# A transformer decoder layer on one core: keys by split products in rows, probabilities turned in other banks

## The chip, the cores and the metric

One Trainium2 chip, one of its cores. The metric is the device time of one execution in microseconds; lower is better. The kernel before takes 476.71 us (median of 3 runs, 476.16 to 478.13).

## What is computed

```python
x = x + xattn(layernorm(x), ctx_1024, fside, mask)   # 16 heads of 32, 4 x 128 queries, 4 x 2048 keys, 512 wide
x = x + attn(layernorm(x))                           # self attention with clamps
x = x + ffn(layernorm(x))                            # 8 experts, each takes its best 32 tokens of a batch, 512-2048-512, gelu
# xattn: q = t @ Wq.T + bq;  k, v = m @ Wkv.T + b;  softmax(q k / sqrt(32) + bias + pad) v @ out_w.T + out_b
```

All is float32. The padding mask lets through only the keys at the end of each batch's context, so that of the 64 chunks of 128 keys only those that hold such a key need any work: 11 chunks with these inputs.

## The kernel before

The instructions of each engine are written out by hand in one block per engine, and semaphores order them. There is no planner: the order in each engine's block is the order of its work.

**Split products.** Where a product needs more than one rounding to the matmul's fast 32-bit type (`F32R`), both operands are held as a high half (a cast, by ScalarE) and a low half (operand minus high half, by VectorE), and TensorE adds three products: high by high, high by low, low by high. `split_att(n)` (L411 on ScalarE, L678 on VectorE) does that for one 512x512 weight matrix, `split_chunk(t)` (L471, L732) for the context chunk `ctx_s`, `project_t` and `project` (L1133, L1150) use the halves. `k_project` (L1098) doesn't: it multiplies plain float32, `wk_s` by `ctx_s`, in 16 matmuls of 128 columns, each of which the trace shows as two records, and gets the keys already turned (features in partitions).

**Start.** x is loaded and normalised, turned by TensorE (`turn_batch`), and the queries of all 512 rows are projected (`project_t`, 4 groups of 12 matmuls of 512 columns, into PSUM banks 0 to 3). VectorE evacuates each group twice (`queries`, L748): 128 columns for the first batch into `q_now`, and all 512 into `qt`. VectorE also adds the output bias to x (L758), four instructions. `scores(0)` waits for all of `q_now` and `q_out`. After it come the values of chunk 0 (`v_project`, L1107, four blocks of 3 matmuls of 512 columns into bank 5).

**Chunk loop.** Z below is the start of `scores` of a chunk. In `chunk(t)` (L1216) TensorE does, in this order: keys of chunk t+1 (bank 4, `pk`), the turning back of the attended values of chunk t-1 (`turn_values`, L1209), and then blocks of the values of t+1 between the turning of the probabilities of t (`turn_probs`, L1188, a group of four heads each), `scores(t+1)` (L1167) and `values(t)` (L1195). Probabilities are turned in place: into the score banks 0 to 3 they came from, and VectorE (groups 0 to 2, L803) and ScalarE (group 3, `turned_last`, L439) copy them to `big_b`. So `scores(t+1)`, which writes the same banks, waits for all of these copies. ScalarE's order (L452): exponents of groups 0 and 1 (8 pairs of instructions), the copy of the attended values (`turned_out`, L434), the rescaling factor, exponents of groups 2 and 3, `turned_last`, and the cast of the next context chunk. VectorE's order (`chunk`, L834): two maxima of 8 heads each (L784) with the new running maximum (L787), values evacuated (L729), context low half (L735), changes of the maxima (L792, L794), attended values added to the state (L813), keys evacuated with their bias (L740), state rescaled (L801), turned probabilities 0, 1, 2 (L806), sums (L818, L821). GpSimd copies the queries of the next chunk's batch to `q_now` after each `scores` (L367). SyncE loads the mask rows and the next context chunk; the SyncE and ScalarE queues each issue loads of their own.

`chunk(t)` is run once for t = 0, in a hardware loop for 8 chunks (t = 1 to 8), and once more for the last but one chunk (t = 9) with the normalisation of the first two batches mixed in (`at_end`). A tail (L873 on) does the last chunk together with the output projection of the cross attention. Then come self attention, the routing, and the eight experts, whose weight tiles (`w_tile`, 1 MB each) are loaded by SyncE over the attention's weights (L297 for the first expert) and first cast by ScalarE in `split_first` (L530).

PSUM banks 0 to 3 are `ps`, 4 is `pk`, 5 `pv`, 6 and 7 `po[:, 0]` and `po[:, 1]`. `turn_values` writes bank 7.

## Time and profile before

| | |
|---|---|
| median of 3 runs | 476.71 us |
| the profiled execution | 477.78 us, of which its span is 476.1 us |
| PE busy | 436.1 us (92%) |
| VectorE busy | 371.5 us (78%) |
| ScalarE busy | 294.0 us (62%) |
| GpSimd busy | 81.3 us (17%) |
| bytes moved | 81.99 MB, mean 172 GB/s |

The span goes from the first to the last recorded instruction of one profiled execution; the device time has 1.7 us around it. A matmul's record ends when its result is written, and the next one starts before that: the pace of a row of matmuls is read from the starts. The start, with the first scores, takes until about 33 us, the chunks until about 156 us, the rest of the attention until about 247 us, the routing until 266 us, and the experts the rest.

### The profile page before, as it was taken

What the parts mean: (1) busy time and instruction counts of PE and PEld (TensorE: products, weight loads), DVE (VectorE), ACT (ScalarE), POOL (GpSimd) and SP (SyncE); (2) the same over time, 40 slices, a digit from 0 to 9 for tenths busy, and PEclk for the clock granted to TensorE, in tenths of its full rate; (3) what the DMA queues carried; (4) which work ended last, traced back from release to release, by engine and by line L of the source; (5) the groups of instructions that cost most, each with busy time, mean ns of one, the idle gap of its engine ahead of it and who ended that gap; (6) DMA issues with size and microseconds to landing.
All of it is one profiled execution on the core that took longest, in us unless ns stands there. A gap on an engine that the chain in (4) does not pass through costs nothing. (4 is left out here: it accounts for less than half of the span.)

```text
span 476.1 us, 9610 instructions
## 1 busy us (share of the span) xinstructions
PE 436.1 (92%) x3323; PEld 361.0 (76%) x3323; DVE 371.5 (78%) x500; ACT 294.0 (62%) x600; POOL 81.3 (17%) x88
## 2 busy tenths in 40 slices
PE   1979999999998999989966799999999999999993
PEld 1858888888887779878855688787878787878782
DVE  5796666777778885758877779898989898898963
ACT  1436666666666743567240587778787878777752
POOL 5000000000000022000133141323223140505000
PEclk9999999999999999999987999999999999999998
DMA  8891100000000742610000099999999999898002
GB/s 258 285 337 36 24 24 22 22 22 22 22 22 2 252 147 89 198 70 3 0 2 0 22 393 387 386 381 356 334 348 322 344 319 380 290 382 296 0 0 88
DMA packets 42959, 81.99 MB, mean 172 GB/s; under 512 B 3000, under 2 KB 3128, under 8 KB 42936
## 3 DMA queue, kind: packets, MB, share of 16 engines
q1 hardware_dynamic: 38744, 75.85, 45.5%
q10 hardware_dynamic: 4192, 5.83, 3.7%
q8 instruction: 14, 0.23, 0.2%
q14 instruction: 9, 0.07, 0.0%
HBM read 80.58 MB, written 1.10 MB: 172 GB/s over the span
## 5 line engine op out<-in xcount | busy, mean ns | idle before, releaser
L1059 DVE TENSOR_TENSOR w_lo<-att_w,w_hi 128x2048 fp32r<-128x2048 f32 x60 | 137.8, 2306 | 23.4 <-ACT w_hi L604 23.4
L604 ACT CAST w_hi<-att_w 128x2048 fp32r<-128x2048 f32 x60 | 115.0, 1917 | 15.4 <-PE po L1421 15.4
L426 ACT ACTIVATE big_a<-ps,negm 128x128 f32<-128x128 f32 x176 | 62.4, 406 | 21.0 <-DVE negm L787 21.0
L1421 PE MATMUL po<-w_hi,ht_hi 128*128 128x512 f32 x128 | 51.8, 405 | 0.0
L1421 PE MATMUL po<-w_hi,ht_lo 128*128 128x512 f32 x128 | 50.6, 395 | 0.0
L1421 PE MATMUL po<-w_lo,ht_hi 128*128 128x512 f32 x128 | 50.5, 394 | 0.0
L426 ACT ACTIVATION_READ_ACCUMULATOR big_a<-ps,negm 128x1 f32 x176 | 43.4, 247 | 0.0
L1104 PE MATMUL pk<-ctx_s,att_w 128*128 128x128 f32 x352 | 42.1, 278 | 0.3 <-DMA ctx_s<-in_ctx_t 0.3
L1104 PEld LDWEIGHTS pk<-ctx_s,att_w 128*128 128x128 f32 x352 | 40.2, 192 | 2.4 <-issue 2.3
L784 DVE TENSOR_REDUCE mc<-ps 128x8 f32<-128x1024 f32 x22 | 26.8, 1220 | 12.4 <-PE ps L1185 12.4
L1421 PEld LDWEIGHTS po<-w_hi,ht_lo 128*128 128x128 f32 x128 | 24.1, 188 | 5.7
L1421 PEld LDWEIGHTS po<-w_lo,ht_hi 128*128 128x128 f32 x128 | 24.1, 188 | 5.1
L1421 PEld LDWEIGHTS po<-w_hi,ht_hi 128*128 128x128 f32 x128 | 24.1, 188 | 5.0
L367 POOL COPY q_now<-qk 128x512 f32 x10 | 6.6, 662 | 124.0 <-PE ps L1185 124.0
L1421 PE MATMUL pv<-w_hi,xin_hi 128*128 128x512 f32 x64 | 26.0, 406 | 1.5 <-DVE w_lo L927 1.5
L1421 PE MATMUL pk<-w_hi,xin_hi 128*128 128x512 f32 x64 | 26.2, 410 | 0.3 <-DVE xin_lo L1048 0.3
L399 POOL CAST back_now<-state 128x128 fp32r (+1 forms) x8 | 8.6, 1075 | 101.5 <-PE ps L1461 87.6
L1421 PE MATMUL pv<-w_hi,xin_lo 128*128 128x512 f32 x64 | 25.3, 395 | 0.0
L1421 PE MATMUL pk<-w_hi,xin_lo 128*128 128x512 f32 x64 | 25.3, 395 | 0.0
L1421 PE MATMUL pv<-w_lo,xin_hi 128*128 128x512 f32 x64 | 25.2, 394 | 0.0
L1421 PE MATMUL pk<-w_lo,xin_hi 128*128 128x512 f32 x64 | 25.2, 394 | 0.0
L1192 PE MATMUL ps<-ident,big_a 128*128 128x128 f32 x176 | 24.4, 272 | 0.0
(284 smaller groups left out, 983.2 us busy)
## 6 DMA issues: line engine op xcount, KB each, us to landing
att_w<-in_w SPq DMA_DIRECT2D x64, 1024.0 KB, 6.5
ctx_s<-in_ctx_t SPq DMA_DIRECT2D x11, 256.0 KB, 2.6
x_s<-in_x SPq DMA_DIRECT2D x4, 256.0 KB, 3.6
att_w<-in_wq SPq DMA_DIRECT2D x1, 1024.0 KB, 8.4
att_w<-in_wk SPq DMA_DIRECT2D x1, 1024.0 KB, 10.8
att_w<-in_wv SPq DMA_DIRECT2D x1, 1024.0 KB, 8.4
att_w<-in_sv ACTq DMA_DIRECT2D x1, 1024.0 KB, 7.9
att_w<-in_wo ACTq DMA_DIRECT2D x1, 1024.0 KB, 7.5
```

What stands on the lines that cost most here:

```text
L367: g.tensor_copy(q_now[:], qt[:, bass.ds(b, 1)].rearrange("p a k n -> p (a k) n")).then_inc(q_staged, 1)
L399: g.tensor_copy(back_now[:], back[:, bass.ds(e, 1), :].rearrange("p a n -> p (a n)")).then_inc(back_staged, 1)
L426: ins = a.activation(big_a[:, h], ps[:, c, g * P:(g + 1) * P], ACT.Exp, bias=negm[:, h:h + 1], accum_out=sums[:, h:h + 1])
L604: a.copy(w_hi[:, i % SLOTS], att_w[:, i]).then_inc(hi_ok, 1)
L784: v.tensor_reduce(mc[:, hs], ps[:, 2 * half:2 * half + 2].rearrange("p c (g k) -> p (c g) k", k=P), AX.X, ALU.max).then_inc(loop_dve, 1)
L1059: v.tensor_tensor(w_lo[:, i % SLOTS], att_w[:, i], w_hi[:, i % SLOTS], ALU.subtract).then_inc(lo_ok, 1)
L1104: ins = mm(pk[:, g * P:(g + 1) * P], wk_s[:, k, g * P:(g + 1) * P], ctx_s[:, k], start=k == 0, stop=k == KC - 1)
L1192: ins = nc.tensor.transpose(ps[:, c, g * P:(g + 1) * P], big_a[:, c * KC + g], ident[:])
L1421: ins = mm(dst, l, r, start=start and i == 0, stop=i == len(terms) - 1, skip_group_check=True)
```

## The change

Names of weight halves. `att_r` lies on the same bytes as `att_w`: the halves of the key weights go where the query and key weights were, those of the output weights where the value and output weights were.

```diff
+        att_r = halves.enter_context(nc.sbuf_tensor("att_r", [P, 8, KC, D], F32R))
+        keys_s = att_w[:, 6, 1]
+        wk_hi, wk_lo, wo_hi, wo_lo = (att_r[:, i] for i in range(4))
-        SPLITS = ((wq_s, 2, in_wq), (wv_s, 1, in_wv), (sv_s, 3, in_sv), (wo_s, 2, in_wo), (sq_s, 1, in_sq), (sk_s, 0, in_sk), (so_s, 1, in_so))
+        SPLITS = ((wq_s, slot_of(2), in_wq), (wk_s, (wk_hi, wk_lo), in_wk), (wv_s, slot_of(1), in_wv), (sv_s, slot_of(3), in_sv),
+                  (wo_s, (wo_hi, wo_lo), in_wo), (sq_s, slot_of(1), in_sq), (sk_s, slot_of(0), in_sk), (so_s, slot_of(1), in_so))
+        TURNED_PROBS = [7, 4, 7, 4]
```

SyncE, the tiles of the first expert; and GpSimd, ahead of its loop:

```diff
             sp.wait_ge(v_mm, last + 2)
-            sp.wait_ge(att_lo_ok, 4)
-            for i in range(2 * NQ):
+            for i in (0, 1, 4, 2, 3, 5, 6, 7):
                 if i == 4:
-                    sp.wait_ge(att_lo_ok, 5)
+                    sp.wait_ge(att_lo_ok, 6)
+                if i == 2:
+                    sp.wait_ge(o_mm, B)
...
             pool.wait_ge(q_out, 4)
+            pool.wait_ge(in_bo, 16)
+            for b in range(B):
+                g.tensor_tensor(x_s[:, b], x_s[:, b], bo_b[:], ALU.add).then_inc(bo_added, 1)
```

ScalarE before its loop. All weight loads are now issued one after the other, and it makes the full query tiles. In `split_att`, split 1 (keys) waits for the low half of the query weights, split 4 (output) for that of the value weights.

```diff
             load_att(sv_s, sv, in_sv)
-            split_att(1)
             load_att(wo_s, wo, in_wo)
-            split_att(2)
...
-            act.wait_ge(q_mm, KC)
+            split_att(1)
+            split_att(2)
+            def queries(c):
+                act.wait_ge(q_first, c + 1)
+                a.activation(qt[:, :, c], ps[:, c].rearrange("p (b t) -> p b t", b=B), ACT.Identity,
+                             bias=bq_scaled[:, c:c + 1], scale=SCALE).then_inc(q_out, 1)
+            act.wait_ge(bq_ok, 1)
+            queries(0)
             split_att(3)
+            queries(1)
+            split_att(4)
+            queries(2)
+            queries(3)
             split_chunk(1)
```

VectorE before its loop (the low half of the key weights also waits for the first keys) and in `chunk`:

```diff
+            def keys_evacuate(t):
+                dve.wait_ge(k_mm, t + 1)
+                v.tensor_copy(keys_s, pk[:]).then_inc(keys_ok, 1)
...
-                v.tensor_scalar(qt[:, :, c], ps[:, c].rearrange("p (b t) -> p b t", b=B), cols[:, 0, c:c + 1],
-                                SCALE, ALU.add, ALU.mult).then_inc(q_out, 1)
+            split_chunk(0)
+            dve.wait_ge(in_cols, 80)
+            v.tensor_scalar(bq_scaled[:], cols[:, 0], SCALE, None, ALU.mult).then_inc(bq_ok, 1)
+            split_att(1)
             queries(0)
-            dve.wait_ge(in_bo, 16)
-            for b in range(B):
-                ins = v.tensor_tensor(x_s[:, b], x_s[:, b], bo_b[:], ALU.add)
-            link(ins)
+            split_att(2)
+            k_evacuate(0)
             queries(1)
-            split_att(2)
+            split_att(3)
             queries(2)
             queries(3)
-            split_att(3)
+            split_att(4)
...
                 nm = running(neg_max, t)
+                if before is None:
+                    v_evacuate(t)
+                split_chunk(t + 1)
                 maximum(t, nm, 0)
                 maximum(t, nm, 1)
                 if before is not None:
                     dve.wait_ge(pv_mm, t)
-                v_evacuate(t)
-                split_chunk(t + 1)
+                    v_evacuate(t)
                 moved_maxima(t, nm)
+                keys_evacuate(t + 1)
                 if before is not None:
                     add_values(before, t)
                 k_evacuate(t + 1)
+                turned_probs(t, 0, banks[TURNED_PROBS[0]])
+                turned_probs(t, 1, banks[TURNED_PROBS[1]])
                 rescale(t, running(state, t))
...
```

The old places of probabilities 0 and 1 in `chunk` go; 2 and the sums stay behind the rescaling, and in the `at_end` chunk the reciprocals stand between the rescaling and 2. `k_evacuate` now waits for `kt_mm`, the turned keys. TensorE: `k_project(0)` is the old product under the name `first_keys`; the others are new.

```diff
+            def k_project(t):
+                pe.wait_ge(ctx_lo_ok, t + 1)
+                pe.wait_ge(k_out, t)
+                if isinstance(t, int) and t == 1:
+                    pe.wait_ge(att_lo_ok, 2)
+                else:
+                    pe.wait_ge(pt_act, t - 1)
+                product(pk[:], [(c[:, k], w[:, k]) for k in range(KC)
+                                for c, w in ((ctx_hi, wk_hi), (ctx_hi, wk_lo), (ctx_lo, wk_hi))]).then_inc(k_mm, 1)
+            def turn_keys(t):
+                pe.wait_ge(keys_ok, t)
+                for g in range(KC):
+                    ins = nc.tensor.transpose(pk[:, g * P:(g + 1) * P], keys_s[:, g * P:(g + 1) * P], ident[:])
+                ins.then_inc(kt_mm, 1)
...
-                if not isinstance(t, int) or t > 0:
-                    pe.wait_ge(pt_dve, t * 3)
-                    pe.wait_ge(pt_act, t)
...
+            def turn_aside(t, c):
+                if c == 0 and (not isinstance(t, int) or t > 0):
+                    pe.wait_ge(pt_dve, t * 3)
+                if c == 1:
+                    pe.wait_ge(k_out, t + 2)
+                if c >= 2:
+                    pe.wait_ge(pt_dve, t * 3 + (c - 1))
+                turn_probs(t, c, banks[TURNED_PROBS[c]])
...
                 k_project(t + 1)
+                v_project(t + 1, 0)
                 if before:
                     turn_values(t)
-                v_project(t + 1, 0)
-                turn_probs(t, 0)
                 v_project(t + 1, 1)
-                turn_probs(t, 1)
+                turn_keys(t + 1)
+                turn_aside(t, 0)
                 v_project(t + 1, 2)
-                turn_probs(t, 2)
-                turn_probs(t, 3)
+                turn_aside(t, 1)
+                turn_aside(t, 2)
+                turn_aside(t, 3)
                 v_project(t + 1, 3)
                 scores(t + 1)
...
+            pe.wait_ge(att_lo_ok, 3)
+            for k in range(KC):
+                v_project(0, k)
             pe.wait_ge(q_out, 4)
             scores(0)
-            pe.wait_ge(att_lo_ok, 2)
-            for k in range(KC):
-                v_project(0, k)
```

`turn_values` now writes bank 6 (`po[:, 0]`), and `values(t)` waits for `summed` instead of `ot_out`. In the tail the probabilities are still turned in their own banks, and `cross_project` takes the output weights' halves from their new place.

## Rows read from the trace of the kernel before

**Rows 1.** Timeline, GpSimd: the query copies that follow scores 1 and 9
```profile
48.63 0.61 POOL L367 COPY q_now<-qk 128x512 f32 x1 [12.88 <-PE ps L1185]
...
141.47 0.61 POOL L367 COPY q_now<-qk 128x512 f32 x1 [10.99 <-PE ps L1185]
```
**Rows 2.** Timeline, PE, chunk 1: start us, us, instruction, [idle before <-releaser]
```profile
47.15 0.40 PE L1180 MATMUL ps<-bias,ones 32*128 32x512 bf16 x4
...
49.38 3.84 PE L1104 MATMUL pk<-ctx_s,att_w 128*128 128x128 f32 x32
53.51 0.66 PE L1213 MATMUL po<-ident,att_w 128*128 128x128 f32 x4 [0.29 <-ACT att_w L437]
53.92 0.48 PE L1114 MATMUL pv<-w_hi 128*128 128x512 f32 x1
54.24 0.39 PE L1114 MATMUL pv<-w_lo,w_hi 128*128 128x512 f32 x1
...
54.70 0.60 PE L1192 MATMUL ps<-ident,big_a 128*128 128x128 f32 x4
...
56.97 1.03 PE L1192 MATMUL ps<-ident,big_a 128*128 128x128 f32 x8
57.76 0.47 PE L1114 MATMUL pv<-w_hi 128*128 128x512 f32 x1
...
58.77 0.40 PE L1180 MATMUL ps<-bias,ones 32*128 32x512 bf16 x4
```
**Rows 3.** Timeline, VectorE and then ScalarE, the same chunk
```profile
48.50 1.22 DVE L784 TENSOR_REDUCE mc<-ps 128x8 f32<-128x1024 f32 x1 [1.33 <-PE ps L1185]
...
52.03 0.68 DVE L735 TENSOR_TENSOR w_lo<-ctx_s,w_hi 128x512 fp32r<-128x512 f32 x1
52.63 0.17 DVE L792 TENSOR_TENSOR mdiff<-negm,neg_max 128x16 f32<-128x16 f32 x1
...
57.60 0.69 DVE L806 COPY big_b<-ps 128x512 f32<-128x512 f32 x1 [0.21 <-PE ps L1192]
...
50.08 0.37 ACT L426 ACTIVATE big_a<-ps,negm 128x128 f32<-128x128 f32 x1 [2.35 <-DVE negm L787]
...
52.83 0.63 ACT L437 COPY att_w<-po 128x512 f32<-128x512 f32 x1
...
58.04 0.59 ACT L441 COPY big_b<-ps 128x512 f32<-128x512 f32 x1 [1.68 <-PE ps L1192]
58.73 0.62 ACT L475 CAST w_hi<-ctx_s 128x512 fp32r<-128x512 f32 x1
```
**Rows 4.** Timeline, PE, start: first query matmul, scores 0, a value matmul behind it
```profile
18.83 0.50 PE L1130 MATMUL ps<-tr_hi,w_hi 128*128 128x512 f32 x1 [0.16 <-DVE tr_lo L676]
...
33.14 0.40 PE L1180 MATMUL ps<-bias,ones 32*128 32x512 bf16 x4 [2.89 <-DVE qk L752]
...
34.71 0.63 PE L1114 MATMUL pv<-w_lo,w_hi 128*128 128x512 f32 x1
```
**Rows 5.** Stretch 34 to 39 us: busy by engine, clock (0.66), DMA share, GB/s
```profile
34.00:39.00 5.00, 5.00 (x30) 3.93 (x27) 3.89 (x5) 0.00 (x0) 1.10 (x1) 0.66 0.44 151
```
**Rows 6.** One line's instructions: duration ns min/median/max, first and last start
```profile
L415 ACT CAST w_hi<-att_w x7: 1899/1910/1912, 11.2 to 195.8; 128x2048 fp32r<-128x2048 f32 x7
L682 DVE TENSOR_TENSOR w_lo<-att_w,w_hi x7: 2276/2282/2293, 14.1 to 197.7; 128x2048 fp32r<-128x2048 f32 x7
```
**Rows 7.** The same view of a GpSimd line, and one VectorE row beside it
```profile
L387 POOL TENSOR_TENSOR tr_lo<-norm,tr_hi x4: 1261/1270/3191, 247.5 to 253.6; 128x512 fp32r<-128x512 f32 x4
...
252.31 1.21 DVE L1021 TENSOR_TENSOR gsm<-gsm,gred 128x32 f32<-128x32 f32 x1
```
**Rows 8.** Timeline of the tail: PE scores 10, VectorE maximum, PE second turning
```profile
152.53 0.39 PE L1180 MATMUL ps<-bias,ones 32*128 32x512 bf16 x4 [1.02 <-DVE big_b L806]
...
153.90 1.23 DVE L784 TENSOR_REDUCE mc<-ps 128x8 f32<-128x1024 f32 x1 [0.46 <-PE ps L1185]
...
156.09 0.66 PE L1123 MATMUL pk<-ident,norm 128*128 128x128 f32 x4 [0.67 <-DVE tr_lo L676]
```
**Rows 9.** Expert tile loads (KB, us to landing); their fifth issue; first use of tile 2
```profile
att_w<-in_w SPq DMA_DIRECT2D x64, 1024.0 KB, 6.5
...
178.91 0.37 SPq L306 DMA_DIRECT2D att_w<-in_w  x1
...
201.38 1.90 ACT L534 CAST w_hi<-att_w 128x2048 fp32r<-128x2048 f32 x1
```

More of the change, by code:

```diff
@@ L69, in decoder_layer @@
         cols = sb("cols", [P, 4, KC])
+        bq_scaled = sb("bq_scaled", [P, KC])
         gate_s = sb("gate_s", [P, KC, E])
@@ L411, in split_att @@
             def split_att(n):
-                w, slot, landed = SPLITS[n]
+                w, halves, landed = SPLITS[n]
                 act.wait_ge(landed, 16)
-                a.copy(w_hi[:, slot], w).then_inc(att_hi_ok, 1)
+                if n == 1:
+                    act.wait_ge(att_lo_ok, 1)
+                if n == 4:
+                    act.wait_ge(att_lo_ok, 3)
+                a.copy(halves[0], w).then_inc(att_hi_ok, 1)
             def transposed(i, b):
@@ L437, in turned_out, with turned_last @@
                 a.copy(ot_s[:].rearrange("p k t -> p (k t)"), po[:, 0]).then_inc(ot_out, 1)
-            def turned_last(t):
+            def turned_last(t, bank):
                 act.wait_ge(pt_mm, 4 * t + 4)
-                a.copy(big_b[:, 3 * KC:4 * KC].rearrange("p h k -> p (h k)"), ps[:, 3]).then_inc(pt_act, 1)
+                a.copy(big_b[:, 3 * KC:4 * KC].rearrange("p h k -> p (h k)"), bank).then_inc(pt_act, 1)
             def turned_second(t):
@@ L459, in softmax_chunk @@
                 exponents(t, 3)
-                turned_last(t)
+                turned_last(t, banks[TURNED_PROBS[3]])
             act.dma_start(mask_s[:], key_mask).then_inc(in_mask, 16)
@@ L509, in _ @@
             normed_cross(0)
-            turned_last(last)
+            turned_last(last, ps[:, 3])
             transposed(2, 0)
@@ L812, in add_values @@
                 dve.wait_ge(loop_dve, 4 * n)
-                v.tensor_tensor(st, st, po[:, 1], ALU.add).then_inc(summed, 1)
+                v.tensor_tensor(st, st, po[:, 0], ALU.add).then_inc(summed, 1)
             def add_sums(t):
@@ L851, in chunk @@
                     reciprocals(0, 2)
-                turned_probs(t, 1)
+                turned_probs(t, 2, banks[TURNED_PROBS[2]])
                 if at_end:
                     attended(0)
-                turned_probs(t, 2)
                 add_sums(t)
@@ L881, in _ @@
             cross_output(0)
-            turned_probs(last, 0)
+            turned_probs(last, 0, ps[:, 0])
             add_values(prev, last)
@@ L886, in _ @@
             reciprocals(2, 3)
-            dve.wait_ge(pt_mm, 4 * last + 3)
-            v.tensor_copy(big_b[:, 2 * KC:3 * KC].rearrange("p h k -> p (h k)"), ps[:, 2]).then_inc(pt_dve, 1)
+            turned_probs(last, 2, ps[:, 2])
             attended(2)
@@ L902, in _ @@
             transposed(1, 3)
-            split_att(4)
+            split_att(5)
             cross_output(3)
@@ L1096, in _, with first_keys @@
             mm = nc.tensor.matmul
-            def k_project(t):
-                pe.wait_ge(ctx_in, t * 16 + 16)
-                if not isinstance(t, int) or t > 0:
-                    pe.wait_ge(k_out, t)
+            def first_keys():
+                pe.wait_ge(ctx_in, 16)
                 for g in range(KC):
@@ L1148, in project_half, with project @@
                         ins.then_inc(done, 1)
-            def project(slot, b, dst, done):
+            def project(halves, b, dst, done):
                 now = slice(b * T, (b + 1) * T)
-                product(dst, [(t[:, k, now], w[:, slot, k]) for k in range(KC)
-                              for w, t in ((w_hi, tr_hi), (w_lo, tr_hi), (w_hi, tr_lo))]).then_inc(done, 1)
+                hi, lo = halves
+                product(dst, [(t[:, k, now], w[:, k]) for k in range(KC)
+                              for w, t in ((hi, tr_hi), (lo, tr_hi), (hi, tr_lo))]).then_inc(done, 1)
             prime(pe, v_mm, s_mm)
@@ L1186, in scores, with turn_probs @@
                 ins.then_inc(s_mm, 1)
-            def turn_probs(t, c):
+            def turn_probs(t, c, bank):
                 pe.wait_ge(p_ok, t * 4 + (c + 1))
                 for g in range(KC):
-                    ins = nc.tensor.transpose(ps[:, c, g * P:(g + 1) * P], big_a[:, c * KC + g], ident[:])
+                    ins = nc.tensor.transpose(bank[:, g * P:(g + 1) * P], big_a[:, c * KC + g], ident[:])
                 ins.then_inc(pt_mm, 1)
+            def turn_aside(t, c):
[6 more added lines that the diff above has]
+                turn_probs(t, c, banks[TURNED_PROBS[c]])
             def values(t, at_end=False):
@@ L1212, in turn_values @@
                 for g in range(KC):
-                    ins = nc.tensor.transpose(po[:, 1, g * P:(g + 1) * P], ot_s[:, g], ident[:])
+                    ins = nc.tensor.transpose(po[:, 0, g * P:(g + 1) * P], ot_s[:, g], ident[:])
                 ins.then_inc(bt_mm, 1)
@@ L1236, in _ @@
             pe.wait_ge(in_wk, 16)
-            k_project(0)
+            first_keys()
             pe.wait_ge(tr_lo_ok[0], B)
@@ L1264, in _ @@
             pe.wait_ge(v_out, last + 1)
-            pe.wait_ge(att_lo_ok, 4)
+            pe.wait_ge(att_lo_ok, 5)
             cross_project(0)
-            turn_probs(last, 0)
-            turn_probs(last, 1)
+            turn_probs(last, 0, ps[:, 0])
+            turn_probs(last, 1, ps[:, 1])
             cross_project(1)
-            turn_probs(last, 2)
-            turn_probs(last, 3)
+            turn_probs(last, 2, ps[:, 2])
+            turn_probs(last, 3, ps[:, 3])
             turn_batch(2, 0)
```

57 lines of the change are left out of this document (31 added, 26 removed).

## The prediction

> **What bounds the kernel now.** The change touches the start and the chunk loop, so I read those and not the experts. First the GpSimd copies that follow each `scores` [rows 1]: from scores 1 at 48.63 to scores 9 at 141.47 there are 8 periods, (141.47 - 48.63) / 8 = 11.60 us a chunk. Then one chunk in the timelines, all measured from Z = 47.15, the start of `scores` [rows 2, 3]. The reader is to see that PE looks full and is not the limit. It waits for ScalarE's copy of the attended values before `turn_values` (0.29 us, at Z+6.36), and again ahead of the next scores. What sets the period is a chain:
>
> - Z to the first maximum, 1.35 (48.50); maximum to first exponent, 1.58 (50.08); eight exponents, 2.75 (52.83); copy to `turn_values`, 0.68 (53.51). So `turn_values` starts at Z+6.36, whatever PE did before.
> - From there PE works without a gap to the start of the last turning pair (56.97) and its end at 58.00; ScalarE copies group 3 at 58.04 until 58.63; scores at 58.77, Z+11.62. That leg is 5.26.
>
> **Step 1, keys as split products.** The plain product takes 3.84 us [rows 2]. The new one is 12 matmuls of 512 columns. Their pace is (54.70 - 54.24) / 2 = 0.23 us, a block of three takes 0.78 behind a transpose and 0.70 behind another block [rows 2]; so 12 take 0.32 + 11 x 0.23 = 2.85. The turning of the keys adds four transposes, 0.41 after a wait (53.51 to 53.92), about 0.4 in a row (0.79 for eight, 56.97 to 57.76). PE has 3.84 - 2.85 - 0.4 = 0.6 us less work a chunk. This saving lies ahead of the `turn_values` gate: keys end at Z+5.1, the first value block at Z+5.8, and PE then waits until Z+6.36 for ScalarE. All but the 0.29 us of today's wait is nothing gained, and those 0.29 don't set the gate either. Worth zero in the loop. The added key copy on VectorE (as the copy in rows 3, 0.60 from start to next start) stands at Z+5.3, in the stretch where VectorE now waits for `turn_values`; covered. If that cover went, it would add 0.6.
>
> **Step 2, the probabilities in banks 7 and 4.** Scores no longer wait for the copies; instead each turning waits for the bank's last reader. After the gate, PE goes: `turn_values` 0.41, value block 0.78, keys and group 0 turned 0.79, value block 0.78. So group 1 is turned at Z+6.36+2.76 = Z+9.12. Its bank is free: keys are evacuated from Z+8.2 to Z+8.9. VectorE can copy group 1 at 9.12 + 0.63 = 9.75 (four transposes 0.60, pick-up 0.03 as at 57.60 behind 56.97). Group 3 needs that bank: 9.75 + 0.69 + 0.07 = Z+10.51. The exponents of group 3 are done at about Z+9.2 (6.28 behind the first one), earlier, so the copy decides. Then 0.41 for turning, 0.78 for the last value block: next Z at 11.70. The leg behind the gate is 5.34 instead of 5.26: the copy wait is not removed, it is moved one value block forward, and it now goes through VectorE.
>
> **Step 3, context low half moved to the front of VectorE's chunk.** The last value block now runs straight into scores, so its end, which releases ScalarE's cast, comes at Z+0.17 instead of a little before Z (the cast starts at 58.73, 0.04 ahead of Z, now). Cast 0.62, then the subtraction, 0.60 of VectorE's time (52.03 to 52.63) [rows 3]: VectorE is free for the maximum at about Z+1.47, not Z+1.35. That is 0.12 on the chain. `k_project` waits for the low half too, until about Z+1.6, and is reached at Z+2.23 (49.38): covered.
> So the period is 11.70 + 0.12 = 11.82, and 8 periods cost 8 x 0.22 = +1.8 us. Bounds: the handoffs from VectorE to PE were taken as 0.07; if they are none and the subtraction hides, 11.6, +0; if each of the four between gate and scores costs 0.15 more, 12.4, +6.
>
> **Step 4, the start.** Before, PE ends the queries near 30.25 and sits idle 2.89 us until VectorE has evacuated them [rows 4]; after scores 0 at 33.14 the matmuls of the values start 0.43 apart instead of 0.23 (they last 0.63), in a stretch with granted clock 0.66 [rows 4, 5], that is partly at 1.2 GHz. Now the values of chunk 0 fill the gap: 18.83 + 48 x 0.2325 = 30.0, plus 12 x 0.23 = 32.8. Is all ready then? ScalarE issues its loads in one go until about 20.2, casts keys and values weights (1.91 each [rows 6]) by 24.1, makes query tile 0, casts the third by 27.3, and so on in turn; the last query tile is at 31.7. VectorE: key low half 22.1 to 24.4 (2.2 each [rows 6]), values low half by 26.9, third by 30.0, fourth until 32.8. Both in time: scores 0 at 32.8 against 33.14, at full clock. Next ScalarE casts chunk 1 from 33.0 and VectorE subtracts until 34.4, maximum at 34.35, exponents from 35.9. Sixteen exponents and the factor take 2 x 2.75 + 0.28 = 5.8: done 41.7, turning at 41.8, block, scores 1 at 43.0. Before it was 47.15 [rows 2]. Gain 4.15.
>
> **Step 5, x plus bias on GpSimd.** Four adds of 128x512 from 31.7 on. The nearest row is GpSimd's subtraction of that size, 1.27 us, and 3.19 where VectorE's 2.28 us subtraction ran first [rows 7]. The other way round, a VectorE instruction on 32 elements took 1.21 us while these ran [rows 7], some 1.0 more than its neighbours. So the adds run from 32.8 to about 38 and stand in the way of what VectorE does then: the subtraction, two small maxima steps and the change of maxima, all with two inputs in SBUF, all on the chain to the exponents. Nothing at best, 4 x 1.0 at worst; I take 1.0 in all, because VectorE's waits and GpSimd's gaps alternate. The gain of the start is 4.15 - 1.0 = 3.15. The adds themselves have until `cross_output`, 120 us later. The query copy behind them has until 43: covered.
> The Trainium skill, SBUF — State Buffer, Who interferes with whom, says that a VectorE instruction with two SBUF inputs contends with GpSimd reads, and that the order of issue decides who blocks. By that rule alone each of the four could meet an add, and the sum would be at its worst end, 479; the row shows one such meeting and not how often they come.
>
> **Step 6, the tail.** In the last but one chunk (Z at 139.99, 1.48 us ahead of its query copy at 141.47 [rows 1], as 47.15 is of 48.63) scores 10 now waits 1.02 us for the copies [rows 8]; this goes. But VectorE then sets the pace: probabilities 2 move behind rescaling and reciprocals, the key copy and the late front add up, and the maximum of chunk 10, today at Z+13.91, comes at Z+14.3 by the same steps. The second turning, today at Z+16.10, follows it: +0.4. Bounds -0.5 and +1. Loads of expert tiles: the fifth goes at 178.9, then 2 and 3; three at 6.5 each, even one after another, end by 198.4, before tile 2's cast at 201.38 [rows 9]. Zero; without that cover it would be 3 us at most. The cast and subtraction of the output weights merely change places; bq_scaled is four elements.
>
> **The sum.** -3.15 + 1.8 + 0.4 = -1.0 us. Against the profiled execution's own 477.78 that is 476.8; it lay 1.07 above the median, so on the median's scale 475.7.
>
> **Rivals.**
> A, faster: the loop doesn't lengthen and GpSimd meets VectorE rarely: -4.15 + 0 + 0.4 = -3.75, 473.0. For it: PE really has 0.6 us less to do per chunk. Against: the chain through ScalarE to Z+6.36 is untouched, and PE waits there already. Chance 0.33.
> B, slower: the handoffs around banks 7 and 4 cost more. Group 2 waits for copy 0, group 3 for copy 1, keys for their copy, and each wait stands in PE's order ahead of the last value block and scores. With +0.6 a chunk on top of step 2 (12.4), -3.15 + 6.4 + 0.4 = +3.6, 480.3. It decides from a period of 12.3 on: 8 x 0.65 = 5.2 outweighs the start and leaves over 2.4. For it: the copies that had one late reader now have three in line. Against: a PE row follows its releaser by 0.05 to 0.1 in rows 2. Chance 0.12.
> C, the clock: PE's idle time a chunk grows from 0.5 to 1.2 us, in pieces up to 0.7. Against: the granted clock is 1.0 in the loop with today's gaps; only after 2.9 us idle did it fall. If it fell once in the loop, the pace 0.43 instead of 0.23 would cost 9 matmuls behind the gate 1.8 us, and 15 ahead of it 3.0 less the wait of 0.7: 4 us for each chunk, 480. Chance 0.05.
> The skill's TensorE: Matmul & The Clock Gate, HAM oscillation, reports micro-idles from cycling PSUM banks as a cause of re-throttling, and its Part 4 says that transposes don't count as busy. This chunk cycles banks and adds transposes, so that rule speaks for C; the trace of before, with 20 transposes a chunk at clock 1.0, doesn't bear it out.
> My own case, -1.0, has 0.5.
>
> **How the numbers follow.** A measurement of this kernel tells changes above about 0.5%, 2.4 us: faster is below 474.3, slower above 479.1. Case A is all faster (0.33), and my case reaches across that line in few of its values: faster 0.34. B and C are slower: 0.17. Same: 0.49. The predicted time is my case's, 475.7. The range takes in A's 473.0 with the bound of the tail (-0.5 more, 472.5) and reaches up to 479.2, half of the way into B: 472.5 to 479.2. What is left out is the worst of B and C and a start better than computed.
>
> **What would show it.** Right: scores 1 near 44; GpSimd's query copies 11.8 apart; PE idle 0.6 to 0.7 ahead of `turn_values` and 0.5 ahead of the turning of group 3, with VectorE's copy as releaser; the maximum 0.1 later behind Z; clock 1.0 from 18 us on. The small VectorE steps of chunk 0 at over 1 us beside GpSimd's adds. Wrong: query copies 11.3 apart or less (PE was the limit), or 12.3 and more (B); clock below 1 in the loop (C); scores 1 later than 46 (the start gained nothing).

## The result, and the profile after

The changed kernel takes 490.5 us (median of 4 runs, 489.17 to 492.67) against 476.46 for the kernel before in the same comparison (476.16 to 478.13): ratio 1.0295, 95% interval 1.025 to 1.034. It is 14 us slower where 1 us less was forecast; time and direction were both wrong. The profiled execution took 490.2 us with a span of 488.5, 12.4 us above the span before. Two executions of the runs below were slow ones (one of number 10, 1089.13 us, and one of the kernel before beside it, 506.11 us), and the medians and ratios given there leave them out. The busy times of the changed kernel, from the page:

```profile
PE 439.9 (90%) x3163; PEld 350.6 (72%) x3163; DVE 376.2 (77%) x504; ACT 298.8 (61%) x605; POOL 90.3 (18%) x92
```

TensorE's busy time has hardly grown (436.1 before): the time is in waits, and it splits at three landmarks, which the kernel before has in [rows 2], [rows 1] and [rows 8].

**The start, +4.66.** Timeline of ScalarE and of its DMA queue (ACTq), from the first cast of the context on:

```profile
17.20 0.62 ACT L493 CAST w_hi<-ctx_s 128x512 fp32r<-128x512 f32 x1 [0.81 <-issue]
...
18.63 0.78 ACTq L487 DMA_DIRECT2D att_w<-in_sq  x1
19.44 1.30 ACTq L487 DMA_DIRECT2D att_w<-in_sk  x1
20.78 4.35 ACTq L487 DMA_DIRECT2D att_w<-in_so  x1
25.15 2.76 ACTq L506 DMA_DIRECT2D gate_s<-in_gate  x1
28.01 1.91 ACT L433 CAST att_r<-att_w 128x2048 fp32r<-128x2048 f32 x1 [10.19 <-issue]
```

The number behind each start is the duration. The prediction let ScalarE issue its loads until about 20.2. The issue of `so` alone lasted 4.35 us and that of the gate 2.76; ScalarE stood still for 10.19 us, and the first weight cast came at 28.01. TensorE's timeline in the same stretch, and the table of windows (PE, PEld, VectorE, ScalarE, GpSimd, clock, DMA share, GB/s):

```profile
34.76 0.80 PE L1168 MATMUL pv<-w_hi 128*128 128x512 f32 x1 [3.42 <-DVE w_lo L714]
35.35 0.63 PE L1168 MATMUL pv<-w_lo,w_hi 128*128 128x512 f32 x1
...
40.18 0.39 PE L1232 MATMUL ps<-bias,ones 32*128 32x512 bf16 x4
...
51.81 0.40 PE L1232 MATMUL ps<-bias,ones 32*128 32x512 bf16 x4
```
```profile
34.00:39.00 5.00, 4.24 (x10) 3.37 (x11) 5.00 (x7) 4.48 (x5) 0.00 (x0) 0.50 0.29 89
```

The values of chunk 0 were to fill the idle 2.89 us of [rows 4]; they start behind 3.42 us of idle time, and then run 0.43 apart at clock 0.50, the lower level of 1.2 GHz, where [rows 5] had 0.66. Scores 0 come at 40.18 (33.14 before), scores 1 at 51.81 (47.15 before). Some of that is not the change's: the cast of the context, at 17.20 here, is at 16.10 in the trace before, and between 16.30 and 17.84 in the traces of the experiments, whose code is the same up to there. Against that anchor scores 1 come at +34.61 instead of +31.05: 3.56 us later, with the other 1.1 lying ahead of the change. Where starts are compared below, it is from this cast, called the anchor.

**The loop, +6.27.** GpSimd's query copies behind scores 1 and scores 9:

```profile
53.30 0.78 POOL L381 COPY q_now<-qk 128x512 f32 x1 [6.95 <-PE ps L1237]
...
152.41 0.86 POOL L381 COPY q_now<-qk 128x512 f32 x1 [11.42 <-PE ps L1237]
```

(152.41 - 53.30) / 8 = 12.39 us a chunk, against 11.60 [rows 1] and the forecast 11.82. One chunk, Z = 88.89, first VectorE, then ScalarE, then PE (as [rows 3] and [rows 2]):

```profile
90.21 0.69 DVE L767 TENSOR_TENSOR w_lo<-ctx_s,w_hi 128x512 fp32r<-128x512 f32 x1 [0.93 <-ACT w_hi L493]
90.82 1.22 DVE L819 TENSOR_REDUCE mc<-ps 128x8 f32<-128x1024 f32 x1
...
99.21 0.69 DVE L841 COPY big_b<-pk 128x512 f32<-128x512 f32 x1 [0.28 <-PE pk L1244]
```
```profile
89.00 0.62 ACT L493 CAST w_hi<-ctx_s 128x512 fp32r<-128x512 f32 x1
92.38 0.37 ACT L444 ACTIVATE big_a<-ps,negm 128x128 f32<-128x128 f32 x1 [2.76 <-DVE negm L822]
...
95.14 0.62 ACT L455 COPY att_w<-po 128x512 f32<-128x512 f32 x1
```
```profile
88.89 0.40 PE L1232 MATMUL ps<-bias,ones 32*128 32x512 bf16 x4
...
95.81 0.66 PE L1275 MATMUL po<-ident,att_w 128*128 128x128 f32 x4 [0.31 <-ACT att_w L455]
...
98.57 0.60 PE L1244 MATMUL pk<-ident,big_a 128*128 128x128 f32 x4
99.06 0.65 PE L1244 MATMUL po<-ident,big_a 128*128 128x128 f32 x4
100.03 0.65 PE L1244 MATMUL pk<-ident,big_a 128*128 128x128 f32 x4 [0.32 <-DVE big_b L841]
...
101.31 0.40 PE L1232 MATMUL ps<-bias,ones 32*128 32x512 bf16 x4
```

The reader is to see that ScalarE's cast ends at 89.62 and VectorE's subtraction, which waited for it, starts 0.59 later. The row names ScalarE as what ended its wait, but ScalarE had long been done; something else stood between (run 2). So the maximum comes at Z+1.93 instead of Z+1.35; the steps from there (1.56, 2.76, 0.67) are those of before, and `turn_values` starts at Z+6.92 instead of Z+6.36. The leg behind it is 5.50 instead of 5.26. Together +0.80.

**The tail, +1.16.** The second turning of the cross attention comes at 168.18, 17.26 behind scores 9 at 150.92, instead of 16.10 behind. VectorE's maximum of chunk 10 stands 2.19 ahead of it in both traces (153.90 to 156.09 in [rows 8]), so all of the 1.16 lies ahead of that maximum:

```profile
165.99 1.23 DVE L819 TENSOR_REDUCE mc<-ps 128x8 f32<-128x1024 f32 x1
```

It comes at Z+15.07 (Z = 150.92) instead of Z+13.91, and VectorE has no wait left ahead of it, where [rows 8] has one of 0.46. 4.66 + 6.27 + 1.16 = 12.09 of the 12.4 us of the span. The gate projection follows the second turning 80.88 us later here and 80.89 in the trace before; the other 0.3 lies behind it.

### The profile page after: what moved, and what is told of

It reads as the page before. It is cut to its first block and busy times, and to the rows that moved or that the text cites. A ratio compares the mean times of both kernels' runs of the same rounds, so it can differ in the third digit from the quotient of the medians.

```text
span 488.5 us, 9319 instructions
## 1 busy us (share of the span) xinstructions
PE 439.9 (90%) x3163; PEld 350.6 (72%) x3163; DVE 376.2 (77%) x504; ACT 298.8 (61%) x605; POOL 90.3 (18%) x92
## 5 line engine op out<-in xcount | busy, mean ns | idle before, releaser
L1168 PE MATMUL pv<-w_hi 128*128 128x512 f32 x44 | 21.4, 487 | 6.8 <-DVE w_lo L714 3.4
L381 POOL COPY q_now<-qk 128x512 f32 x10 | 9.1, 914 | 98.4 <-PE ps L1237 98.4
L1184 PE MATMUL pk<-att_r,w_hi 128*128 128x512 f32 x80 | 25.8, 403 | 0.8 <-DVE w_lo L767 0.8
L407 POOL COPY x_now<-qk 128x512 f32 x7 | 16.1, 2301 | 41.5 <-PE pv L1485 41.5
```

Of the source, the lines that this page charges most:

```text
L381: g.tensor_copy(q_now[:], qt[:, bass.ds(b, 1)].rearrange("p a k n -> p (a k) n")).then_inc(q_staged, 1)
L407: g.tensor_copy(x_now[:], now).then_inc(x_now_ok, 1)
L1168: ins = mm(pv[:], c[:, k], w[:, 1, k], start=k == 0 and c is ctx_hi and w is w_hi, stop=k == KC - 1 and c is ctx_lo, skip_group_check=True)
L1184: ins = mm(dst, l, r, start=n == 0, stop=n == len(pairs) - 1, skip_group_check=True)
```

## Experiments

Totals of one kernel spread over some 5 us, and the run's mean granted clock goes with them: in 31 runs of the kernel before the fastest, 473.19 us, had 0.988 and the slowest, 478.91, had 0.971. So each experiment is read by positions in its trace first and by its total second. A large part of the spread lies in code that no experiment touches: from the gate projection to the end the traces take between some 238.0 us (runs 2 and 3) and 242.7 (runs 5 and 9). The kernel before had medians of 476.11 beside runs 1 to 4 and 475.60 beside 5 to 8 and beside 9 to 11.

**1. The four loads spread between ScalarE's casts.**

```diff
-            for dst, w, landed in ((sq_s, sq, in_sq), (sk_s, sk, in_sk), (so_s, so, in_so)):
-                load_att(dst, w, landed)
-            act.dma_start(gate_s[:], gate.rearrange("(k p) e -> p k e", p=P)).then_inc(in_gate, 16)
             split_att(1)
             split_att(2)
+            load_att(sq_s, sq, in_sq)
...
             split_att(3)
+            load_att(sk_s, sk, in_sk)
             queries(1)
             split_att(4)
+            load_att(so_s, so, in_so)
             queries(2)
+            act.dma_start(gate_s[:], gate.rearrange("(k p) e -> p k e", p=P)).then_inc(in_gate, 16)
```

> The changed kernel with its last four ScalarE loads (two query-side weights, output weights, gate) issued one by one between the casts instead of in one row. Theory 1 (issue): ScalarE was held by its own load issues until 28.0 us (4.35 us for the fourth, 2.76 us for the gate), so casts, halves and scores 1 came late. Expected: key cast near 19 to 20 us, scores 1 at 44 us instead of 51.8, time 490.5 - 7.8 = about 483, loop period unchanged at 12.4. Rival (arrival): the weights themselves come later because all loads share the bandwidth; then the casts still wait for their loads and scores 1 moves by less than 3 us, 488 or more.

484.89 us (4 runs), ratio 1.0195 (1.0136 to 1.0254). Timeline of ScalarE and its queue:

```profile
17.80 1.90 ACT L433 CAST att_r<-att_w 128x2048 fp32r<-128x2048 f32 x1 [0.88 <-issue]
...
28.52 0.38 ACTq L487 DMA_DIRECT2D att_w<-in_so  x1
29.14 0.37 ACTq L522 DMA_DIRECT2D gate_s<-in_gate  x1
```

The same two issues last 0.38 and 0.37 us instead of 4.35 and 2.76, the first weight cast comes at 17.80, and scores 1 at 44.40, 28.10 behind the anchor: 6.5 us earlier than in the changed kernel. The period stays (12.38 against 12.39). ScalarE's held-up issues were the loss at the start. The total fell by 5.6 and not by the expected 7.8: behind the gate projection this trace takes 241.15 us, that of the changed kernel 239.44.

**2. Context low half ahead of the read of the chunk's table entry.** In the chunk VectorE first reads registers to find its row of `neg_max`; the subtraction was placed behind that.

```diff
-                nm = running(neg_max, t)
                 if before is None:
                     v_evacuate(t)
                 split_chunk(t + 1)
+                nm = running(neg_max, t)
                 maximum(t, nm, 0)
```

> The changed kernel with VectorE's subtraction of the context low half put ahead of the reading of the chunk's batch number (a load from the table in SBUF and address arithmetic) in each pass of the loop. Theory 2 (table read): the subtraction starts 0.6 us after ScalarE's cast because VectorE is still reading the table, which used to be covered by the wait for scores. Expected: the subtraction starts within 0.1 us of the cast's end, the maximum 1.4 to 1.5 us behind the start of scores instead of 1.93, period 11.9 instead of 12.4, time 490.5 - 4.5 = about 486. Rival (handoff): the 0.6 us are the wait on the semaphore or GpSimd's query copy; then nothing moves, 490.5.

486.33 us (4 runs), ratio 1.0221 (1.0165 to 1.0277). Query copies from 53.61 to 149.67, so the period is (149.67 - 53.61) / 8 = 12.01. Moving one line that computes nothing gives back 0.38 us a chunk. GpSimd's copies also last 0.61 again where they lasted some 0.98 (rows of 65.53 to 140.00 in the changed kernel).

**3. Both.**

> Both edits. If theories 1 and 2 hold and the two parts are independent: 490.5 - 7.8 - 4.5 = about 478, scores 1 at 44 us, period 11.9. By both rivals: above 487.

480.22 us (10 runs), ratio 1.0093 (1.0059 to 1.0128). The gains of runs 1 and 2 add up, 490.5 - 5.6 - 4.2 = 480.7; what was too high in the expected 478 was each of them. Scores 1 stand 28.06 behind the anchor, the period is 12.00. Timeline of ScalarE, then VectorE, then PE, Z = 81.48:

```profile
81.58 0.62 ACT L493 CAST w_hi<-ctx_s 128x512 fp32r<-128x512 f32 x1
```
```profile
82.23 0.69 DVE L768 TENSOR_TENSOR w_lo<-ctx_s,w_hi 128x512 fp32r<-128x512 f32 x1 [0.37 <-ACT w_hi L493]
82.98 1.23 DVE L820 TENSOR_REDUCE mc<-ps 128x8 f32<-128x1024 f32 x1
```
```profile
87.98 0.66 PE L1276 MATMUL po<-ident,att_w 128*128 128x128 f32 x4 [0.31 <-ACT att_w L455]
...
93.46 0.40 PE L1233 MATMUL ps<-bias,ones 32*128 32x512 bf16 x4
```

The subtraction now follows the cast by 0.03 (81.58 + 0.62 = 82.20), and the maximum stands at Z+1.50, the forecast being Z+1.47. It starts 0.75 behind the start of the subtraction, in the changed kernel 0.61 (90.21 to 90.82): this fits a read that goes on while the subtraction works and is nearly hidden by it, which is argued and not shown. The leg behind `turn_values` is 93.46 - 87.98 = 5.48, as it was. Even with both repairs the changed loop is 0.4 slower than the old one.

**4. The same without x plus bias.** The output bias is left out of the computation.

```diff
-            for b in range(B):
-                g.tensor_tensor(x_s[:, b], x_s[:, b], bo_b[:], ALU.add).then_inc(bo_added, 1)
```

> Both edits, and the output bias is not added to x at all (left out of the computation). Theory 3 (shared with GpSimd): the four adds make VectorE's small maxima steps of chunk 0 last 1.12 and 0.53 us instead of 0.17; without them scores 1 comes 1.0 to 1.3 us earlier than in the kernel with both edits, the rest unchanged. Rival: the adds run beside VectorE at no cost to the path; scores 1 does not move.

480.24 us (8 runs), ratio 1.0096 (1.0055 to 1.0136). Scores 1 come 27.04 behind the anchor instead of 28.06: the adds cost 1.0 us there. The total, with its spread, does not show it. What it is made of stands in the changed kernel's timeline, GpSimd's four adds and the query copy behind them, and two small VectorE steps beside these:

```profile
39.40 6.40 POOL L377 TENSOR_TENSOR x_s<-x_s,bo_b 128x512 f32<-128x512 f32 x4 [26.94 <-ACT qk L513]
45.76 0.60 POOL L381 COPY q_now<-qk 128x512 f32 x1
```
```profile
43.45 1.12 DVE L822 SCALAR_TENSOR_TENSOR negm<-mc,neg_max 128x8 f32<-128x8 f32 x1 [0.16 <-DVE mc L819]
...
45.86 0.53 DVE L822 SCALAR_TENSOR_TENSOR negm<-mc,neg_max 128x8 f32<-128x8 f32 x1
```

In run 4 both steps take 0.17 us. The prediction weighed a rule of the Trainium skill (SBUF — State Buffer, Who interferes with whom), that a VectorE instruction with two SBUF inputs contends with GpSimd's reads; the trace agrees with it. But not all four steps met an add: the first of these two lost 0.95 beside the adds and the subtraction 0.17 (0.86 at 41.31), the second lost 0.36 beside the query copy, which the adds had pushed there, and the change of maxima, at 46.42, came behind both and lost nothing.

**5. The new start alone, in the kernel before.** Query tiles by ScalarE with the scaled bias, values of chunk 0 ahead of scores 0, loads between the casts; the loop is the old one.

```diff
+            act.wait_ge(bq_ok, 1)
+            queries(0)
             split_att(2)
-            for dst, w, landed in ((sq_s, sq, in_sq), (sk_s, sk, in_sk), (so_s, so, in_so)):
-                load_att(dst, w, landed)
+            load_att(sq_s, sq, in_sq)
+            queries(1)
+            load_att(sk_s, sk, in_sk)
+            queries(2)
+            load_att(so_s, so, in_so)
...
-            pe.wait_ge(q_out, 4)
-            scores(0)
             pe.wait_ge(att_lo_ok, 2)
             for k in range(KC):
                 v_project(0, k)
+            pe.wait_ge(q_out, 4)
+            scores(0)
```

> The kernel before with only the new start: full query tiles by ScalarE, the values of chunk 0 ahead of scores 0, loads issued between the casts; the loop, the keys and the bias adds as before. Theory 1: the start alone is a gain of about 4 us: scores 0 at 32.8 us, scores 1 at 43.2 instead of 47.15, clock 1.0 there, period 11.60, time 476.1 - 3.9 = about 472. Rival: the start's gain needs the new loop's order or is taken back at the first chunk; scores 1 at 46 or later, 475 or more.

477.53 us (10 runs), ratio 1.0032 (0.9997 to 1.0067): no gain in the total, where 3.9 us were expected. Yet scores 1 stand 27.82 behind the anchor (31.05 before), 3.2 us earlier, the period is 11.60, and the gate projection comes at 235.15 instead of 236.98, although the anchor stands 1.4 later in this trace. Where the gain goes is seen from two rows of each trace, the table of windows for 240 to 250 and 250 to 260 us (columns as above), of the kernel before and then of this one:

```profile
240.00:250.00 10.00, 7.43 (x40) 6.22 (x40) 7.80 (x13) 5.23 (x8) 3.62 (x3) 0.81 0.01 2
250.00:260.00 10.00, 6.20 (x21) 4.49 (x20) 7.12 (x24) 0.23 (x1) 4.47 (x4) 0.67 0.00 0
```
```profile
240.00:250.00 10.00, 8.08 (x38) 6.82 (x37) 6.13 (x9) 5.04 (x7) 3.89 (x3) 0.67 0.00 1
250.00:260.00 10.00, 7.00 (x19) 4.99 (x20) 7.29 (x25) 0.23 (x1) 4.19 (x4) 0.50 0.00 0
```

The change does not touch this code, and its granted clock was lower in both stretches. From the first gate projection to the second it took 7.50 us (235.15 to 242.65) instead of 5.94 (236.98 to 242.92), as the matmuls from 238.61 to 241.59 started 0.43 apart, where those of the kernel before started 0.23 apart. That makes 18.15 us instead of 16.60 to the first matmul of the choice of experts, and from there to the end it took 224.5 instead of 222.5. PE's idle times just ahead of the slower matmuls were those of the kernel before (0.97 and 0.49 against 0.98 and 0.50). The traces of runs 7, 9 and 11 have some 18.15 in the same place too, those of runs 2 and 3 have 15.2. What decides it was not found; that stays open.

**6. The probabilities turned in place again.** As 3, with banks 0 to 3, scores waiting for the copies as before, and the rescaling behind the third copy.

```diff
-        TURNED_PROBS = [7, 4, 7, 4]
+        TURNED_PROBS = [0, 1, 2, 3]
...
                 pe.wait_ge(k_out, t + 1)
+                if not isinstance(t, int) or t > 0:
+                    pe.wait_ge(pt_dve, t * 3)
+                    pe.wait_ge(pt_act, t)
...
-                rescale(t, running(state, t))
                 turned_probs(t, 2, banks[TURNED_PROBS[2]])
+                rescale(t, running(state, t))
```

> The kernel with both edits, probabilities turned in their own banks 0 to 3 again, scores waiting for the four copies, VectorE's rescaling behind the third copy. Theory 4 (bank handoff): the loop's leg behind turn_values is set by group 1's copy, which group 3 waits for; in place, all four groups are turned in a row and the period falls from 12.0 to 11.3, below the 11.6 of before; time 480.2 - 5.6 = about 474.6. Rival (copies late): scores wait as long for the copies as the turnings did for the banks; period 11.9 to 12.1, time 480.

480.45 us (10 runs), ratio 1.0091 (1.0057 to 1.0125): the total of run 3, not the 474.6 that was expected. The leg behind `turn_values` shrank from 5.48 to 5.00 (87.08 to 92.08), but the period only from 12.00 to (140.85 - 46.65) / 8 = 11.78, where 11.3 was expected (the first is 11.38, the others some 11.83), because VectorE is late for the next chunk:

```profile
92.77 0.17 DVE L857 TENSOR_TENSOR total<-total,sums 128x16 f32 x1
93.16 0.69 DVE L768 TENSOR_TENSOR w_lo<-ctx_s,w_hi 128x512 fp32r<-128x512 f32 x1 [0.21 <-issue]
93.91 1.22 DVE L820 TENSOR_REDUCE mc<-ps 128x8 f32<-128x1024 f32 x1
```

Three copies, the rescaling and the sums end at 92.94, and the maximum is at Z+1.83. With the subtraction standing ahead of the maximum, what VectorE finishes late is on the chain. The 2 us that the loop gains don't reach the total, because the tail of this trace takes them back. PE's second turning, and the window from 156 to 170 us:

```profile
156.86 0.95 PE L1176 MATMUL pk<-ident,norm 128*128 128x128 f32 x4 [2.00 <-DVE tr_lo L707]
```
```profile
156.00:170.00 14.00, 12.67 (x91) 10.75 (x92) 10.64 (x24) 9.92 (x40) 0.74 (x2) 0.88 0.52 190
```

The turning comes 5.79 behind scores 10 (151.07) instead of 4.98 in run 3, behind 2.00 us of idle time, and the granted clock of this window is 0.88, where run 3 had 1.00. From this turning to the one at 172.99 it then takes 16.13 us, in run 3 14.52 (158.45 to 172.97).

**7. The same with the bias adds on VectorE, where they were before.**

```diff
-            for b in range(B):
-                g.tensor_tensor(x_s[:, b], x_s[:, b], bo_b[:], ALU.add).then_inc(bo_added, 1)
...
+            dve.wait_ge(in_bo, 16)
+            for b in range(B):
+                ins = v.tensor_tensor(x_s[:, b], x_s[:, b], bo_b[:], ALU.add)
+            link(ins)
             split_att(2)
```

> The same with the four bias adds back on VectorE between the first query tile and the low half of the value weights, where it waits for loads and PE. Theory 3 (shared with GpSimd) gives 1.0 us less than the kernel in place: about 473.6. Rival: 2.5 us of VectorE work at the start push the last weight half beyond scores 0; scores 1 comes 1 us later instead of earlier, 475.6.

478.03 us (10 runs), ratio 1.0029 (1.0 to 1.0058). Scores 1 stand 27.27 behind the anchor (28.17 in run 6): 0.9 earlier, the price of the adds once more; the rival, that they delay the weight halves, falls. The total fell by 2.4, more than the adds explain: in this trace the stretch for which run 6 took 16.13 us takes 14.53 (155.37 to 169.90), at clock 1.00.

**8. Less work for TensorE.** As 3, with the product of the context's low half left out of the keys of all chunks but the first: 8 matmuls of 512 columns instead of 12.

```diff
-                                for c, w in ((ctx_hi, wk_hi), (ctx_hi, wk_lo), (ctx_lo, wk_hi))]).then_inc(k_mm, 1)
+                                for c, w in ((ctx_hi, wk_hi), (ctx_hi, wk_lo))]).then_inc(k_mm, 1)
```

> The kernel with both edits, the keys of chunks 1 to 10 without the low half of the context (4 of 12 matmuls left out): PE has 0.93 us less to do in each chunk, all of it ahead of turn_values. Theory 5 (chain): the period stays 12.0, because turn_values waits for ScalarE; time 480. Rival (PE-bound): the period falls by 0.9 to 11.1, time 472.

480.49 us (8 runs), ratio 1.0113 (1.0079 to 1.0147); the period stays (11.99 against 12.00), and scores 1 stand 28.05 behind the anchor. Some 0.9 us less (4 x 0.23) for TensorE ahead of `turn_values` are worth nothing, so TensorE is not the bound there.

**9. ScalarE's copy of the attended values ahead of the exponents.** If the chain through that copy is what counts, it can be cut: the values are ready at about Z+2.3, when ScalarE is idle. The kernel is number 5 and this:

```diff
+                if before:
+                    turned_out(t)
                 exponents(t, 0)
                 exponents(t, 1)
-                if before:
-                    turned_out(t)
```

> The kernel before with the new start (as in the run with the start alone) and ScalarE's copy of the attended values ahead of the exponents of its chunk instead of behind eight of them; TensorE's order is untouched. Theory (the period is set by a gate that sixteen ScalarE instructions stand in front of): the copy fits into ScalarE's idle 2.3 us, delays the first exponent by 0.1 at most, and turn_values follows the keys without its wait of 0.28; the period falls from 11.60 to 11.3, and the gate projection, at 235.15 with the start alone, comes at about 232.3. Total 474.5 to 476. Rival (the wait is only handed on, to the copy of group 3 or to VectorE): period 11.5 to 11.6, gate projection at 234.5 or later, total as with the start alone, 477.5.

472.91 us (9 runs), ratio 0.992 (0.9884 to 0.9956). The period is (136.05 - 47.22) / 8 = 11.10. ScalarE and PE, one chunk:

```profile
81.42 0.59 ACT L438 COPY att_w<-po 128x512 f32<-128x512 f32 x1 [1.78 <-PE po L1218]
81.97 0.37 ACT L427 ACTIVATE big_a<-ps,negm 128x128 f32<-128x128 f32 x1
```
```profile
81.28 3.84 PE L1117 MATMUL pk<-ctx_s,att_w 128*128 128x128 f32 x32
84.95 0.60 PE L1226 MATMUL po<-ident,att_w 128*128 128x128 f32 x4
...
90.15 0.40 PE L1193 MATMUL ps<-bias,ones 32*128 32x512 bf16 x4
```

`turn_values` starts at Z+5.90 (Z = 90.15 - 11.10 = 79.05) instead of Z+6.36, with no wait, and the leg behind it is 5.20. The gain, 0.5, is more than the 0.28 that the wait showed: PE starts `turn_values` 3.67 behind the keys here and 4.13 behind them in [rows 2], which is 0.46 for a wait written as 0.29. The end in a matmul's record is modelled and lies behind the start of the next one, so a wait of the next one is shown short. The period fell by 0.5 and the total by 4.6 against run 5, where 0.3 and 1.5 to 3 were expected.

**10. The same move in the changed kernel with both repairs** (number 3).

> The kernel with both repairs (loads between casts, low half before the table read) and the same move of ScalarE's copy. Theory: what turn_values waits for there (0.31 us) goes, the leg from scores to turn_values shrinks from 6.50 to 6.2, the rest stands: period 11.7 instead of 12.0. Rival (VectorE's queue around the aside banks sets the pace there): adding the attended values starts no earlier, period 11.9 to 12.0.

475.70 us (11 runs), ratio 0.9998 (0.997 to 1.0026). The period is (138.18 - 46.38) / 8 = 11.48, 0.52 less than in 3 (11.7 was expected), so both loops had the same gate. What is left of the change's cost, 11.48 against 11.10, no longer hangs on it. The one wait that PE still shows in such a chunk is that of group 3 for a bank:

```profile
89.53 0.65 PE L1245 MATMUL pk<-ident,big_a 128*128 128x128 f32 x4 [0.33 <-DVE big_b L842]
```

**11. As 9, and in chunk 0 the low half between the two maxima.**

```diff
                 maximum(t, nm, 0)
+                if before is None:
+                    v_evacuate(t)
+                    split_chunk(t + 1)
                 maximum(t, nm, 1)
                 if before is not None:
                     dve.wait_ge(pv_mm, t)
-                v_evacuate(t)
-                split_chunk(t + 1)
+                    v_evacuate(t)
+                    split_chunk(t + 1)
```

> As e9_copy_ahead, and in chunk 0 alone VectorE evacuates the values and subtracts the low half between the two maxima instead of behind them. TensorE's wait of 1.11 us ahead of the first value block of chunk 1 (at 40.41 with the start alone) should go; scores 1 then wait for the exponents and come 0.8 earlier (44.5 instead of 45.28). Rival: the second maximum, 1.2 later, delays the factor and with it eight exponents by as much, and scores 1 come no earlier than 45.2.

471.78 us (7 runs), ratio 0.9904 (0.9868 to 0.994), the best version. Scores 1 stand 27.67 behind the anchor against 27.90 in 9: 0.2 instead of the 0.8 expected. TensorE's wait of 1.1 us is gone, but a new one stands in its place, as the rival said:

```profile
42.86 0.66 PE L1208 MATMUL ps<-ident,big_a 128*128 128x128 f32 x4 [0.74 <-ACT big_a L427]
```

The intervals of 9 and 11 overlap; that 11 is better than 9 is not shown.

## Why the prediction was wrong, step by step

- **Step 1, keys as split products: right.** The saving was put at nothing in the loop, and run 8 shows that even 0.9 us less moves nothing. Its size was read too high, which cost nothing: the plain product occupies PE for 3.67 (start to start, run 9) and not for the 3.84 of its record, so that 0.4 are saved and not 0.6.
- **Step 2, banks 7 and 4: right in kind, too small in size.** Forecast 5.34 for the leg behind the gate, measured 5.50 (5.48 in run 3). Up to the turning of group 1 the forecast stood (2.76). The steps behind it did not: from VectorE's copy of group 1 to the turning of group 3 it takes 0.82 (99.21 to 100.03), not 0.76, and from there to scores 0.41 + 0.87, not 0.41 + 0.78. That is the +0.16 by which this term of the sum was mis-sized. Run 6 shows the other side: turned in place, the leg is 5.00.
- **Step 3, low half at the front: the step that failed in the loop.** It priced the cast and the subtraction, +0.12, and nothing between them. Measured +0.58 (Z+1.93 for Z+1.35). The register read that finds the chunk's row had been hidden in VectorE's wait of 1.33 for scores [rows 3]; once a longer piece of work stands behind it, it is on the chain. Run 2 moves it behind that work and 0.38 a chunk comes back; run 3 then has +0.15, close to the +0.12 of the text. Eight periods make this the largest part of the loop's +6.27.
- **Step 4, the start: the step that failed first.** "ScalarE issues its loads in one go until about 20.2" names no row. In the trace before, ScalarE's seven issues behind the anchor take 4.00 us together, which from 16.11 on gives the 20.2 with the small gaps between. Four of them, three loads and the gate, stood in one row there as well:

```profile
24.44 0.37 ACTq L469 DMA_DIRECT2D att_w<-in_sq  x1
24.85 0.98 ACTq L469 DMA_DIRECT2D att_w<-in_sk  x1
25.86 0.53 ACTq L469 DMA_DIRECT2D att_w<-in_so  x1
26.42 0.91 ACTq L490 DMA_DIRECT2D gate_s<-in_gate  x1
```

  What failed is that the row of all seven was to last no longer than that. In it the last three lasted 1.30, 4.35 and 2.76 us, and the first cast came 7.8 later than that sentence says (1.1 of it the anchor's). All the rest of the step holds once the loads stand apart: forecast gain with the adds 3.15, measured 31.05 - 28.06 = 2.99 (run 3); without the adds 4.15 and 31.05 - 27.04 = 4.01 (run 4).
- **Step 5, the adds: right, the size in part by luck.** 1.0 taken, 1.02 and 0.9 measured (runs 4 and 7). It was a choice between 0 and 4.0; the reason given, that waits and gaps alternate, is not what the rows show: one step lost 0.95 beside the adds, and one 0.36 beside the copy behind them.
- **Step 6, the tail: mis-sized.** +0.4 forecast, +1.16 measured, just above the bound of +1. The maximum of chunk 10 was put at Z+14.3 and stands at Z+15.07; the turning follows it by 2.19, as it did before. About 0.3 of it is the lateness of step 3: with both repairs (run 3) the second turning comes 158.45 - 141.47 = 16.98 behind scores 9. The rest stays: from scores 10 to that turning it is 4.98 there (153.47 to 158.45) instead of 3.56 [rows 8]. Which of the instructions that were moved behind the rescaling makes it was not tried.
- **The rivals.** B had the direction and, by chance, nearly the period (12.4), but not the cause: most of the addition lies ahead of the gate. C fell: the clock is 1.00 in the loop, with 24 transposes a chunk and PE waits of 0.3 to 0.4, so the rule of the Trainium skill (TensorE: Matmul & The Clock Gate, A second HAM failure mode: psum-queue depth-cycling) is not borne out by this trace. The reason given against C, that the clock fell only after 2.9 us idle, holds for the start alone: in the same trace it is 0.81 from 240 to 250 us, where no idle time of PE is over 1.24. A held in one respect: the new start can gain nearly its 4.15, with the loads apart and the adds on VectorE 31.05 - 27.27 = 3.78 (run 7).

By these steps the forecast of -1.0 becomes: start +3.56 where -3.15 stood, with 1.1 of drift ahead of it; loop +6.27 for +1.8; tail +1.16 for +0.4. The range failed because both large errors were costs that no row of the trace before showed on the path, issues of several microseconds and a register read under cover, and no bound was set for either.

## What to carry to other kernels

When loads are gathered that stood apart, their issues need not last as long as they did: here ScalarE was held by the last ones of seven in one row, so keep such issues between pieces of the engine's own work. When work is moved to the front of an engine's chunk, ask what already stands there under the cover of a wait, the reads of registers too. And a wait on a chain is a thing to cut rather than to shorten: moving ScalarE's copy over eight exponents into idle time gave 0.5 us a chunk in both loops, and nothing of this change shortened the loop.

## What was not expected of the hardware

- An issue of a 1 MB load from ScalarE lasted 0.38 us with its neighbours apart and 4.35 as the last of five in a row, and ScalarE's casts had to wait for the whole row. In the row of three of the trace before the longest took 0.98.
- GpSimd's copy of 128x512 took 0.98 us instead of 0.61 in the chunks in which VectorE's subtraction, two inputs in SBUF, started just ahead of it (90.21 and 90.39), and 0.61 where the subtraction had ended before it started (82.23 + 0.69 = 82.92, copy at 82.97, run 3).
- Behind the first gate projection the granted clock was 0.81 in one trace and 0.67 in another (240 to 250 us), in kernels that are the same there and with nearly the same idle times ahead, worth 1.56 us up to the second gate projection alone.
